# Query and output products as half-height pairs, and score maxima turned by VectorE

## The reference

```python
x = x + tanh(g_xattn) * attn(layernorm(x), ctx)   # attn below
    q = (xn @ Wq.T)   # 32 heads of 16
    k, v = ctx @ Wk.T, ctx @ Wv.T   # 8 groups of 16, each serves 4 heads
    score = q @ k.T / 4 ; p = softmax(score) ; o = p @ v
    out = o @ Wfc.T + bfc
x = x + tanh(g_ffn) * (shared_mlp(layernorm(x)) + top2_weight * routed_mlp(layernorm(x)))
```

## Time and profile before

| | us |
|---|---|
| median of 3 runs | 889.33 (889.10 to 889.56) |
| the profiled execution | 890.05 |
| its span | 887.7 |
| start to the first step | 44.9 |
| first block | 74.3 |
| second and third block, each | 73.6 |
| last block, to its last step's start | 57.1 |

### The profile page before, as it was taken

How to read it: one execution, slowest core, us unless ns; L and a number is a source line. 1 busy time by engine, 2 the same in 40 slices (tenths; PEclk the granted TensorE clock), 3 DMA queues, 4 the chain that set the end, 5 groups by cost and what they waited for, 6 DMA issues and landing times.

```text
span 887.7 us, 14887 instructions
## 1 busy us (share of the span) xinstructions
PE 860.1 (97%) x4923; PEld 642.5 (72%) x4923; DVE 635.8 (72%) x1085; ACT 337.2 (38%) x636; POOL 477.8 (54%) x485
## 2 busy tenths in 40 slices
PE   8689999999999889999999999999999999999998
PEld 6445665665565447888888888888788888888886
DVE  7789899889889966666556655679665566656565
ACT  4186576667657852122112211344211121112111
POOL 2313004001203999787668666954966696678640
PEclk9889999999999999999999999999999999999999
DMA  7763342432432113121112111211311112111102
GB/s 274 232 175 105 127 121 61 149 116 78 131 107 74 38 28 93 48 72 47 47 47 71 47 47 47 72 47 65 115 59 48 47 52 66 47 47 47 47 1 95
DMA packets 43609, 71.88 MB, mean 81 GB/s; under 512 B 6064, under 2 KB 21936, under 8 KB 43312
## 3 DMA queue, kind: packets, MB, share of 16 engines
q1 hardware_dynamic: 43568, 71.34, 25.5%
HBM read 55.33 MB, written 15.73 MB: 80 GB/s over the span
## 4 chain that ended last, share of the span: by engine, by line
PE 84%; DVE 11%; issue 2%; ACT 1%; DMA 1%; SPq 0%; DVEq 0%; ACTq 0%
PE bank L1293 24%; PE bank L1295 23%; PE bank L1294 23%; DVE mcol L906 5%; PE bank L1353 4%; PE bank L1378 4%; PE bank L1368 3%; PE bank L1298 2%; PE bank L1399 1%; DVE oN L1038 1%; ACT probs L761 1%; DVE oB L1028 1%; DVE x_l L1256 1%; DVE aT_l L881 0%; DMA q_scr<-qx_l 0%
## 5 line engine op out<-in xcount | busy, mean ns | idle before, releaser
L1293 PE MATMUL bank<-x_l,w_h 128*128 128x512 f32 x504 | 197.3, 391 | 0.3 <-DVE c L1116 0.3
L1294 PE MATMUL bank<-x_h,w_l 128*128 128x512 f32 x504 | 196.2, 389 | 0.0
L1295 PE MATMUL bank<-x_h,w_h 128*128 128x512 f32 x504 | 196.2, 389 | 0.0
L906 DVE TENSOR_REDUCE mcol<-bank 128x2 f32<-128x512 f32 x256 | 164.7, 671 | 24.8 <-PE bank L1353 24.3
L620 ACT ACTIVATE hT_h<-bank 128x512 fp32r<-128x512 f32 x72 | 43.1, 599 | 355.9 <-DVE bank L1231 347.2
L761 ACT ACTIVATE probs<-bank 128x512 f32<-128x512 f32 x256 | 138.9, 596 | 73.3 <-PE bank L1368 71.7
L572 POOL TENSOR_TENSOR w_l<-raw,w_h 128x512 fp32r<-128x512 f32 (+1 forms) x144 | 161.9, 1157 | 2.9
L1128 DVE SCALAR_TENSOR_TENSOR xa<-bank,tgf,xa 128x512 f32<-128x512 f32 x128 | 96.2, 751 | 77.7 <-PE bank L1295 77.5
L1293 PE MATMUL bank<-dn_l,hT_h 128*128 128x512 f32 x288 | 112.0, 389 | 0.0
L1294 PE MATMUL bank<-dn_h,hT_l 128*128 128x512 f32 x288 | 112.0, 389 | 0.0
L1295 PE MATMUL bank<-dn_h,hT_h 128*128 128x512 f32 x288 | 112.0, 389 | 0.0
(11 more groups left out here) (149 smaller groups left out, 1340.6 us busy)
## 6 DMA issues: line engine op xcount, KB each, us to landing
raw<-w_gu SPq DMA_DIRECT2D x36, 512.0 KB, 3.3
dnraw<-w_dn SPq DMA_DIRECT2D x36, 256.0 KB, 2.6
q_st<-q_scr SPq DMA_DIRECT2D x64, 128.0 KB, 2.7
q_scr<-qx_h SPq DMA_DIRECT2D x16, 256.0 KB, 2.2
q_scr<-qx_l SPq DMA_DIRECT2D x16, 256.0 KB, 2.2
q_st<-q_scr SPq DMA_DIRECT2D x64, 64.0 KB, 2.7
out<-xa SPq DMA_DIRECT2D x16, 256.0 KB, 2.0
cx_raw<-ctxT SPq DMA_DIRECT2D x14, 256.0 KB, 3.0
```

The costliest lines, as they stand in the source:

```text
L906: v.tensor_reduce(at[:, :, qt], sm_bank(n, s, u)[:, :].rearrange("p (r k) -> p r k", r=2), AX.X, ALU.max).then_inc(max_ok, 1)
L1293: mm(out, a_h, b_l, start=start, stop=False, skip_group_check=onto)
L1294: mm(out, a_l, b_h, start=False, stop=False, skip_group_check=onto)
L1295: return mm(out, a_h, b_h, start=False, stop=stop, skip_group_check=onto)
```

## The change

It does four things.

1. In all blocks but the last, the query and the output products are made by `q_both` and `f_both`. A product of 128 rows is cut into two of 64 rows. `both` issues the half on rows 0 to 63 for one output (bank PJ[0]) and the half on rows 64 to 127 for the other output (PJ[1]); later, with `turned`, the halves change over and are added. For the queries the two outputs are two parts of 128 features, for the output products the two halves of the tokens. New semaphores half_q, half_f0, half_f1 stand between the straight and the turned half. The last block's `f_part` stays.
2. These pairs, the x transposes, keys and values are spread over the slots in another order, with some pairs in slot 2. `vt_place` puts the turned v into the second half of the bank that collects the value products (OTB), so `vt_job` waits for `o_turn` (ob_ok). VectorE and ScalarE take `x_low`, `x_high`, `q_low`, `q_high`, `f_sum` and `f_stats` two at a time at other places; SP writes two query parts at once.
3. `mt_job` and `m_copy` go. `turn_maxima` transposes 32 columns of `mcol` to `mT` on VectorE after the first maximum of a step. That gives four lots of 32 tokens, so `put_max` issues four DMAs from 16 partitions to two rows of `q_st`.
4. The constant row of `k_st` is -1 in place of the negation in the copy.

```diff
             def put_max(n, slot):
-                sp.wait_ge(mt_cp, n + 1)
-                for e in range(2):
-                    at = e * ROWS + MROW
-                    sp.dma_start(r(q_st[at:at + 1, slot, :, :].rearrange("p h (t q) -> p (h t) q", q=P)),
-                                 r(mT[e * HC:(e + 1) * HC, :])).then_inc(m_rd, 16)
+                sp.wait_ge(mt_ok, n + 1)
+                for j in range(4):
+                    lot = 32 * j
+                    sp.dma_start(r(q_st[MROW:MROW + ROWS + 1:ROWS, slot, :, :].rearrange("e h (t j q) -> e (h t) j q",
+                                                                                       j=4, q=32)[:, :, j, :]),
+                                 r(mT[lot:lot + 16, slot % 2, :])).then_inc(m_rd[slot % 2], 16)
...
-                    if s >= 4 and not last:
+                    if s in (4, 6) and not last:
                         write_q(t + 1, s - 4)
+                        write_q(t + 1, s - 3)
...
+            def turn_maxima(n, par):
+
+                dve.wait_ge(max_ok, UNITS * (n + 1))
+                if not (isinstance(n, int) and n < 2):
+                    dve.wait_ge(m_rd[par], 32 * (n - par))
+                v.transpose(mT[:, par, :].bitcast(f32),
+                            mcol[:, par, :].bitcast(f32)).then_inc(mt_ok, 1)
...
-                        if not last and (s, u) in ((1, 0), (2, 0)):
-                            x_low(nx, 2 * s - 1)
+                        if u == 0 and (not last or s + 1 < STEPS):
+                            turn_maxima(n + 1, (s + 1) % 2)
+
+                        if not last and (s, u) in ((2, 0), (2, 4)):
+                            x_low(nx, u // 2)
+                            x_low(nx, u // 2 + 1)
...
+                            if s == 0 and u == 0:
+                                for qt in range(2):
+                                    f_sum(t - 1, 0, qt, False)
+                            if (s, u) in (((1, 3), (2, 4)) if last else ((1, 5), (1, 6))):
+                                f_sum(t - 1, 1, s - 1 if last else u - 5, last)
...
+                        if (s, u) in ((5, 0), (6, 4)):
+                            q_low(nx, 2 * (s - 5))
+                            q_low(nx, 2 * (s - 5) + 1)
...
+            def both(out, a_h, a_l, b_h, b_l, turned, start, stop):
+                last = [None, None]
+                for k, (a, b) in enumerate(((a_h, b_l), (a_l, b_h), (a_h, b_h))):
+                    for e in range(2):
+                        rows, i = slice(e * ROWS, (e + 1) * ROWS), 1 - e if turned else e
+                        last[e] = mm(out[i], a(rows, i), b(rows, i), start=start and k == 0, stop=stop and k == 2,
+                                     skip_group_check=True)
+                return last
...
+                            if s == 0 and v == 1:
+                                pe.wait_ge(f_add, TILES * t - 2)
+                                f_both(t - 1, 1, (0, 1, 2), False, start=True, done=half_f1)
+                            if s == 0 and v == 3:
+                                pe.wait_ge(half_f1, 4 * t - 2)
+                                f_both(t - 1, 1, (0, 1, 2), True)
+                            if s == 1 and v == 1:
+                                f_both(t - 1, 1, (3,), True, done=half_f1)
+                        if s == 1 and v == 3:
...
+                                pe.wait_ge(f_add, TILES * t)
                             x_job(nx, 0)
                             x_job(nx, 1)
```

More of the change, by code:

```diff
@@ L1338, in f_part, with q_both, weights, tokens @@
                     last.then_inc(f_mm, 1)
+            def both(out, a_h, a_l, b_h, b_l, turned, start, stop):
[6 more added lines that the diff above has]
+                return last
+            def q_both(tb, o, chunks, turned, start=False, stop=False, done=None):
+                def weights(tile, c):
+                    return lambda rows, i: tile[rows, c, (o + i) * P:(o + i + 1) * P]
+                def tokens(tile, c):
+                    return lambda rows, i: tile[rows, c, :]
+                for c in chunks:
+                    last = both((PJ[0][:, :], PJ[1][:, :]), weights(wq_h, c), weights(wq_l, c), tokens(xnT_h, c),
+                                tokens(xnT_l, c), turned, start and c == chunks[0], stop and c == chunks[-1])
+                for one in last if done else ():
+                    one.then_inc(done, 1)
+            def f_both(t, bb, chunks, turned, start=False, stop=False, done=None):
+                def results(tile, c):
+                    return lambda rows, i: tile[rows, c, i * P:(i + 1) * P]
+                def weights(tile, c):
+                    return lambda rows, i: tile[rows, c, :]
+                for c in chunks:
+                    pe.wait_ge(a_lo, STEPS * t + CHUNKS * bb + c + 1)
+                    last = both((PJ[0][:, :], PJ[1][:, :]), results(a_split[True][bb], c), results(a_split[False][bb], c),
+                                weights(wfc_h, c), weights(wfc_l, c), turned, start and c == chunks[0],
+                                stop and c == chunks[-1])
+                for one in last if done else ():
+                    one.then_inc(done, 1)
             def sm_pair(n, s, v, bb, c):
@@ L1463, in body @@
                                 pv_unit(n - 1, p, (s - 1) % STEPS // CHUNKS, (s - 1) % CHUNKS)
+                        if not first and not last and (s, v) == (1, 2):
+                            pe.wait_ge(half_f1, 4 * t)
+                            f_both(t - 1, 1, (3,), False, stop=True, done=f_mm)
+                        if not last and (s, v) == (5, 2):
+                            q_both(nx, 2, (2, 3), False, done=half_q)
+                        if not last and (s, v) == (7, 2):
+                            pe.wait_ge(half_f0, 2 * t + 2)
+                            f_both(t, 0, (0, 1), True)
                         if v == 2:
@@ L1581, in body @@
+                            q_both(nx, 2, (0, 1), False, start=True)
                         if s == 5 and v == 3:
-                            for c4 in range(1, DC):
-                                q_part(nx, 2, c4)
+                            pe.wait_ge(half_q, CHUNKS * t + 4)
+                            q_both(nx, 2, (0, 1), True)
                         if s == 6 and v == 1:
-                            f_part(t, 0, 0, 1)
-                            f_part(t, 0, 0, 2)
+                            pe.wait_ge(ob_ok, n)
```

204 lines of the change are left out of this document (79 added, 125 removed).

## The result

The changed kernel takes 894.2 us (median of 8 runs, 892.29 to 898.63) against 889.15 (8 runs, 887.09 to 889.56): a ratio of 1.0073, 95% interval 1.0059 to 1.0087. It is slower by about 0.7%. Its runs also scatter more, over 6.3 us where the kernel before has 2.5. Three runs lie at 892.3 to 892.8 with a mean granted clock of 0.989, three at 897.2 to 898.6 with 0.977 to 0.981.

A forecast was written before the change was run, and what follows sets the result against it. TensorE was taken to bound most steps, VectorE near its limit, with waits returning the savings: first block -0.3, two steady blocks +0.75 each, last block +2.7, total +3.9 on 889.33, giving 893.2 us, range 890 to 897.

The forecast's parts named there:

- first block with its lead-in: First block and the stretch ahead of it: savings and late VectorE work together give -0.3 us.
- steady block: Each of two steady blocks: 5.4 us taken off TensorE come back as waits, sum 74.35, +0.75 us.
- last block: Last block keeps single products; VectorE, its bound, gets two sums, a late start and six turns: +2.7 us.
- Steps 0, 1, 2: Steady block: waits for output sums, output turn and x splits make these steps 9.4, 8.8 and 10.7 us.
- Rival (1): The bunching is hidden: steps take their longer sum plus old friction, steady blocks 69.1, total 879 us; chance 0.20.
- Steps 4 and 5: Steady block: SP queue's reads and four maxima DMAs at 0.68 each, then landing, set 9.4 and 10.1 us.
- Rival (2): The four maxima DMAs cost 0.42 us each, not 0.68; total 888.6 us, no change; chance 0.22.
- Steps 3, 6 and 7: Steady block: 8.95 us ruled by TensorE, 8.95 with two exponentials held up by query copies, and 8.05.
- the 7 that I had named as a sign: Sign of a right forecast: steady block near 74 us with TensorE busy 7 us less.
- The gain of 0.41 for a stretch: Slots with only pairs cost TensorE 0.41 us less each; eleven of sixteen give -4.5 us a block.
- Rival (3): The pairs do not pack: each takes 0.34 us, about +22, total 915 us; chance 0.05.
- rival (4): First block: the clock stays low one step longer and step 1's TensorE work doubles, +2 to +3, 896 us; chance 0.08.

The follow-up runs named there:

- half_splits: Changed kernel with the third and fourth x split of each later block at half width; run once for its profile, step 2 falls by 0.30 us.
- old_head: Changed kernel with the order of the kernel before in steps 0 to 2 and pairs from step 3 on; 889.62 us, ratio 1.0014.
- pairs_undone: Changed kernel in its new order, but each pair of half-height products is one full-height product; 899.91 us, ratio 1.0125.
- fill: Changed kernel with four more 512-column products of dead data in step 0 of the first block; 892.97 us, ratio 1.0044.
- fetch_shift: Changed kernel with six warming products left out and 90 tiny ones added, moving TensorE's later program by 84 products; 897.16 us, ratio 1.0091.
- small_sums: Changed kernel with the two output sums in step 0 of the last block covering only 32 of 512 columns; 892.72 us, ratio 1.0064.
- turn_alone: Kernel before with the maxima's part of the change alone, products and their order as before; 887.72 us, ratio 0.9993.
- combined: Changed kernel with the old order in steps 0 to 2, and two of the maxima's four DMAs ahead of the reads in steps 4 and 5; 888.47 us, ratio 0.9989.
- put_split: Changed kernel with two of the maxima's four DMAs issued ahead of the query reads in steps 4 and 5, except last block; 893.57 us, ratio 1.0058.

## Why the prediction came out right, and where it was wrong

Forecast 893.2, measured 894.2, ratio 1.0073 where +0.44% was said. The sign and the size are right, and the chains named for the steady block are those found. But that the total comes so near is partly luck: it said 1.9 too much for the two steady blocks and the last one, and left out 2.4 in the first and a loss in the second that it did not have at all. The parts, as the profiled run of 898.63 has them:

| | said | measured |
|---|---|---|
| first block with its lead-in | -0.3 | +2.1 |
| steady block | +0.75 | +0.16 |
| second block's extra | none | up to +4.4 |
| last block | +2.7 | +2.0 |

*Steady block.* Steps 0, 1, 2 were said to take 9.4, 8.8, 10.7 and take 9.45, 8.87, 10.61. The waits named there are the ones that the third block shows:

```profile
PE bank L1310 <- DVE oB L1041: 1.6, 2, 1.4
PE bank L1310 <- DVE xa L927: 1.4, 1, 1.4
PE bank L1361 <- DVE xa L927: 0.6, 1, 0.6
...
PE bank L1305 <- DVE xnT_l L883: 0.2, 1, 0.2
```

The value transpose waits for the output turn (1.4 the longest), the x transposes and the output pairs for the output sums (1.4 and 0.6), the first key product for the last split (0.2). half_splits and old_head confirm them: step 2 falls with the splits, and the block falls by 1.4 once its old head is back. Rival (1) needed step 2 under 9.6; it is out. Steps 4 and 5 were said to take 9.4 and 10.1 and take 8.53 and 9.49. The chain named is the right one for step 5: the four issues end at 254.63 and the step at 255.72, 0.56 behind the start of the scores where 0.32 is usual. In step 4 the maxima land just when TensorE is ready (0.32 behind the scores). Two terms were too large: an issue takes 0.54, not 0.68, and from the last issue's end to the first product it is 1.1, where I had 1.4 and 2.0. Rival (2) was nearer for these two steps. The step of mine that failed is taking the old form's price for the new form. The Trainium skill, "DMA: Bandwidth & Descriptors" (Why a DMA increments its semaphore by 16 and not by 1), says that a transfer over fewer than 16 engines leaves the issuing queue a semaphore write of its own to do; by that the new form would stay dear. The trace agrees in part: 0.54 against 0.32 to 0.39 for the others, yet well under the 0.68 of the earlier trace rows. Steps 3, 6 and 7 were 0.2 to 0.4 too short in my sum. TensorE's busy time fell by 3.3 us (72.32 to 69.05), not by the 7 that I had named as a sign.

*Pairs.* The gain of 0.41 for a stretch is confirmed where it can be read. In step 4, slot 1, six pairs take 1.95 from scores to scores (160.75 to 162.70), and the next scores' way to the transposed ones is 0.24; with full products the same is 2.26 and 0.34, together 0.41 more. Rival (3) is out. What the steps kept of it is 2.4 a block, by pairs_undone. My sum took 4.5 off TensorE for them and let 5.4, the turn's share too, and 0.75 more come back as waits. Measured are 2.4 saved by the pairs, 0.6 by the turn and 3.2 lost by the order: gain and loss were both said too large, and nearly cancel in either account.

*First block.* I gave rival (4), the clock, 0.08 and a place of its own; it happened together with the forecast. The table of stretches had the row for it: step 0 at a granted clock of 0.57, with two x transposes of 1.06 each that the change takes away. I priced them as work saved (-0.7) and not as the work behind which the clock rose. The full clock came at 63.1, not 53.0, and step 1 took 10.84, not the 8.5 of my sum: that one step is nearly the whole miss of 2.4. fill backs the cause by giving TensorE other work, within the limit that fetch_shift sets (above).

*Second block.* No step of the prediction had it. It looked at queue time and landings as constants. The kernel before has such packets too (at 160.1 and 174.0 in its steps 4 and 6) and room in its queue for them: its second block takes what its third takes. In the changed kernel a packet meets the chain that I had said has no slack. In the profiled run the clock fell behind the stand-still, and that is the larger part (step 6, +2.8). In fill and old_head step 5 was nearly as long (10.85 and 11.13) and the clock stayed at 1.00, so this part comes and goes.

*Last block.* +2.7 was said, +2.0 came. The two sums are 1.0 (small_sums), not 1.3. My sum missed a third operation that moved in: the statistics of an output tile (`f_stats`, 0.68 long), before in step 7 of the block ahead, now stand in step 0 of the last block, where VectorE has 26 operations instead of 22. A turn takes VectorE 0.13 (218.59 to 218.72), not 0.15, and turn_alone shows that in this block it costs nothing that can be seen (57.14 against 57.11).

```profile
218.59 0.20 DVE L916 STREAM_TRANSPOSE mT<-mcol 128x32 f32<-128x32 f32 x1
218.72 1.25 DVE L883 TENSOR_TENSOR xnT_l<-bank,xnT_h 128x512 fp32r<-128x512 f32 x2
```

Open: why the landing of the write in the second block was late; why VectorE's busy time in a steady block stayed at 66.0 although eight turns came in; and how much of the scatter of the changed kernel's unprofiled runs is the same fall of the clock; their mean clocks (0.977 to 0.989) fit it, but only profiled runs show the place.

## What to carry to other kernels

Price a cheaper instruction together with the order that it demands: here half-height pairs save 2.4 us a block and the order that gives them two banks at once takes 3.2; keeping the old order wherever the pairs don't need the new one took the loss away (old_head 1.0014, combined 0.9989). Work taken off TensorE while its clock is low is not a saving before it is known what brings the clock up. And a queue that a sum shows to be just in time is a risk beyond the sum: compare two passes of the same loop to see what an outside delay does to it.

## What the runs showed of the hardware

- Half-height 512-column products on the two halves of the rows start 3 to 4 ns apart (160.9 to 163 us of the changed kernel), and pairs follow each other, and the 48- and 49-row scores on either side, at 0.23 to 0.24 us. The changes to and from full height cost 0.34, twice each time.
- Packets of 16 KB of the instruction queue q8, TensorE's by fetch_shift, come 8 to 20 us apart in the first two blocks of these kernels. In the third, the second pass of the same loop, only turn_alone and put_split show one, near its end. A read or write that the SP queue issues from 0.2 us ahead to 0.5 us behind a packet can take 1.1 to 1.7 us instead of 0.3 to 0.4 (1.22 at 167.6 in the changed kernel, 1.62 at 159.0 in fetch_shift); an issue of the maxima at such a moment took its usual 0.5 (fill, at 125.0). Both halves of a query part were written 4.1 to 4.5 us after the issue of the low half, instead of some 2.4, in seven cases with a packet 0.2 to 1.9 us behind that issue (two each in combined, fetch_shift and turn_alone, one in old_head); in two others, both with the packet at 1.9, they took 2.0 and 2.2.
- The granted clock fell from full speed to 0.50 right behind a stretch in which TensorE stood still for 1.2 us and then 0.4, and came back after 6.9 us of work without a break. A stand-still alone is not enough: in fetch_shift TensorE stood still at the same place for 1.95 and 0.45 us and kept the full clock. In the first block the clock stayed at 0.50 through a step in which TensorE was busy for 7.50 of 9.05 and rose late in the next one (10.46 of 10.84).
